# Landmark inverse: the symmetric product K V as its own stationary operand, its transposed product left out, the first bracket taken from the copy

## The reference

```python
def iterative_inv(K, n_iter=6):
    I = jnp.eye(K.shape[-1], dtype=K.dtype)
    denom = jnp.max(jnp.sum(K, axis=-2), axis=-1)[..., None, None]
    V = jnp.swapaxes(K, -1, -2) / denom
    for _ in range(n_iter):
        KV = K @ V
        V = 0.25 * V @ (13.0 * I - KV @ (15.0 * I - KV @ (7.0 * I - KV)))
    return V
...
SV = kernel1 @ iterative_inv(kernel2) @ (kernel3 @ V)
```

## Time and profile before

| | us |
|---|---|
| median of 3 runs | 6197.68 |
| lowest and highest of them | 6192.51 and 6201.0 |
| the profiled execution | 6204.73 |
| its span | 6202.7 |
| stage L2B in it, about | 2727 to 2842 |

### The profile page before, as it was taken

One profiled execution on the slowest core, in us unless ns is written; L12 is line 12 of the kernel. 1 busy time (PEld: TensorE's weight loads), 2 busy tenths in 40 slices (PEclk: granted clock), 3 DMA queues, 4 the chain that ended last, 5 costly groups with the idle time before them and its releaser, 6 DMA issues. The chain is left out here.

```text
span 6202.7 us, 126873 instructions
## 1 busy us (share of the span) xinstructions
PE 5537.1 (89%) x43980; PEld 3071.1 (50%) x43980; DVE 3363.8 (54%) x4908; ACT 2454.3 (40%) x3318; POOL 2574.7 (42%) x2473
## 2 busy tenths in 40 slices
PE   8569999999997798899689699999999978789996
PEld 6463333333335333779458233333333328778885
DVE  4237777777774697545553466666666634621112
ACT  2225555555552221333422355555555541122221
POOL 0036556555651396331301555555555530161032
PEclk9689999999999898999799899999999999789998
DMA  4863344434433422000026433333333347476675
GB/s 144 258 202 94 90 92 94 93 91 92 95 80 81 136 88 58 25 2 2 5 61 198 120 108 107 104 108 108 104 108 106 104 151 236 166 240 225 205 235 176
DMA packets 840068, 742.62 MB, mean 120 GB/s; under 512 B 514917, under 2 KB 722597, under 8 KB 828966
## 3 DMA queue, kind: packets, MB, share of 16 engines
q1 hardware_dynamic: 827302, 711.16, 39.5%
q0 software_dynamic: 12288, 25.18, 1.2%
HBM read 464.33 MB, written 278.00 MB: 120 GB/s over the span
## 5 line engine op out<-in xcount | busy, mean ns | idle before, releaser
L1186 DVE TENSOR_REDUCE L3B_nmax<-L3B_R 128x1 bf16<-128x1024 f32 x768 | 941.1, 1227 | 635.1 <-PE L3B_R L1080 635.1
L1186 DVE TENSOR_REDUCE L0B_nmax<-L0B_R 128x1 bf16<-128x1024 f32 x768 | 937.0, 1222 | 392.5 <-PE L0B_R L1080 378.5
L1172 ACT ACTIVATE L0B_PT<-L0B_R 128x1024 f32<-128x1024 f32 x768 | 786.6, 1025 | 671.7 <-PE L0B_R L1090 642.8
L1172 ACT ACTIVATE L3B_PT<-L3B_R 128x1024 f32<-128x1024 f32 x768 | 753.3, 1024 | 575.9 <-PE L3B_R L1090 575.9
L1090 PE MATMUL L0B_R<-L0B_QS,L0B_KS 64*128 64x512 bf16 (+1 forms) x6144 | 804.6, 382 | 45.8 <-issue 39.1
L1116 PE MATMUL L3B_O<-L3B_PT,L3B_VA 128*64 128x512 f32 x3072 | 743.6, 605 | 0.0
L1090 PE MATMUL L3B_R<-L3B_QS,L3B_KS 64*128 64x512 bf16 (+1 forms) x6144 | 730.8, 377 | 2.9 <-DMA L3B_QS<-scr_max 2.9
L1090 PEld LDWEIGHTS L0B_R<-L0B_QS,L0B_KS 64*128 64x128 bf16 (+1 forms) x6144 | 260.8, 94 | 511.1 <-issue 207.1
L1090 PEld LDWEIGHTS L3B_R<-L3B_QS,L3B_KS 64*128 64x128 bf16 (+1 forms) x6144 | 299.3, 94 | 329.7 <-ACT L3B_PT L1172 5.7
L1111 PE MATMUL L0B_O<-L0B_PT,L0B_VA 128*32 128x256 f32 x6144 | 422.1, 392 | 1.2 <-issue 1.0
L3236 ACT ACTIVATE L3F_hidden<-L3F_H,L3F_weights 128x256 f32<-128x256 f32 x474 | 182.1, 484 | 488.7 <-PE L3F_H L3168 488.7
(11 more groups left out here) (397 smaller groups left out, 8499.9 us busy)
## 6 DMA issues: line engine op xcount, KB each, us to landing
L3F_weights<-in_L3F_w SPq DMA_DIRECT2D x79, 1251.0 KB, 5.9
scr_sumsL<-L3B_OT SPq DMA_DIRECT2D x96, 512.0 KB
L3C_sums<-scr_sumsL SPq DMA_DIRECT2D x96, 512.0 KB, 9.4
scr_rel<-L0R_terms SPq DMA_DIRECT2D x64, 384.0 KB
L0B_raw<-scr_rel SPq DMA_DIRECT2D x192, 128.0 KB
L3B_raw<-scr_rel SPq DMA_DIRECT2D x384, 64.0 KB
scr_parts<-L0B_qk_parts SPq DMA_DIRECT2D x96, 224.0 KB, 2.3
scr_parts<-L3B_qk_parts SPq DMA_DIRECT2D x96, 224.0 KB, 2.2
```

Source lines behind the costliest of these rows:

```text
L1172: nc.scalar.activation(PT[:, (8 * u + j) % NPT, :, :], score_pair(u, j), ACT.Exp).then_inc(s_exp, 1)
L1186: nc.vector.tensor_reduce(nmax[:, u % 2, 4 * t:4 * t + 1], pair.rearrange("p j n -> p (j n)"), AX, ALU.max, negate=True).then_inc(s_mx, 1)
```

## The change

Product 1, the transposed K V, is left out. ScalarE copies product 0 instead, to `KV`, and `KV` is the stationary operand of the two products that had `KVT`. The first bracket is no longer made from PSUM but from that copy in SBUF, so VectorE waits for ScalarE and TensorE for VectorE there. An iteration has five products, numbered on through all iterations so that the two sets of PSUM banks go on taking turns. The hardware loops are written out: six times the body in the program's text, with constants in the waits.

```diff
-        def out(p, c):
-            return ps[:, p % 2, c, 0:GC * CG].rearrange("p (g n) -> p g n", g=GC)
+        def out(n, c):
+            return ps[:, n % 2, c, 0:GC * CG].rearrange("p (g n) -> p g n", g=GC)
+
+        def made(eng, n, c):
+
+            eng.wait_ge(s_pe, 2 * NC_ + NC_ * n + c + 1)
...
-            with pe.Fori(0, ITER) as it:
-                a0, d0 = it * 12, it * 12
+            for it in range(ITER):
+                n = 5 * it
                 for c in range(NC_):
-                    pe.wait_ge(s_a, a0 + 4 + c + 1)
-                    product(0, c, K2T, V)
+                    pe.wait_ge(s_a, 12 * it + 4 + c + 1)
+                    product(n, c, K2T, V)
                 for c in range(NC_):
-                    pe.wait_ge(s_a, a0 + 8 + c + 1)
-                    product(1, c, V, K2T)
+                    pe.wait_ge(s_a, 12 * it + 8 + c + 1)
+                    pe.wait_ge(s_d, 12 * it + c + 1)
+                    product(n + 1, c, KV, A)
                 for c in range(NC_):
-                    pe.wait_ge(s_a, a0 + 12 + c + 1)
-                    pe.wait_ge(s_d, d0 + 12 + c + 1)
-                    product(2, c, KVT, A)
+                    pe.wait_ge(s_d, 12 * it + 4 + c + 1)
+                    product(n + 2, c, KV, A)
                 for c in range(NC_):
-                    pe.wait_ge(s_d, d0 + 16 + c + 1)
-                    product(3, c, KVT, A)
+                    pe.wait_ge(s_d, 12 * it + 8 + c + 1)
+                    product(n + 3, c, VT, A)
                 for c in range(NC_):
-                    pe.wait_ge(s_d, d0 + 20 + c + 1)
-                    product(4, c, VT, A)
-                for c in range(NC_):
-                    product(5, c, A, VT)
+                    product(n + 4, c, A, VT)
...
-            with act.Fori(0, ITER) as it:
+            for it in range(ITER):
                 for c in range(NC_):
-                    act.wait_ge(s_pe, it * 24 + PRE + 4 + c + 1)
-                    nc.scalar.copy(chunk(KVT, c), out(1, c)).then_inc(s_a, 1)
-                for p, dst in ((4, V), (5, VT)):
+                    made(act, 5 * it, c)
+                    nc.scalar.copy(chunk(KV, c), out(5 * it, c)).then_inc(s_a, 1)
+                for p, dst in ((3, V), (4, VT)):
...
-            dve.sem_inc(s_d, 12)
-            with dve.Fori(0, ITER) as it:
-                for e, p in enumerate((0, 2, 3)):
+            def combine(c, src, e):
+                nc.vector.scalar_tensor_tensor(out=chunk(A, c), in0=src, scalar=-1.0, in1=bc(eyes[:, e, :], 1, GC),
+                                               op0=ALU.mult, op1=ALU.add).then_inc(s_d, 1)
+
+            for it in range(ITER):
+                for c in range(NC_):
+                    dve.wait_ge(s_a, 12 * it + 12 + c + 1)
+                    combine(c, chunk(KV, c), 0)
+                for p in (1, 2):
                     for c in range(NC_):
-                        dve.wait_ge(s_pe, it * 24 + PRE + 4 * p + c + 1)
+                        made(dve, 5 * it + p, c)
+                        combine(c, out(5 * it + p, c), p)
```

More of the change, by code:

```diff
@@ L2160, in landmark_inverse @@
         ps = st.ps("ps", [CG, 2, NC_, 512])
-        K2T, V, VT, KVT, A = (st.sb(n, [CG, NGRP, CG]) for n in ("K2T", "V", "VT", "KVT", "A"))
+        K2T, V, VT, KV, A = (st.sb(n, [CG, NGRP, CG]) for n in ("K2T", "V", "VT", "KV", "A"))
         eyes = st.sb("eyes", [CG, 3, CG])
@@ L2181, in _ @@
             sp.dma_start(own[:, :], cst["block1"]).then_inc(s_w, 16)
-        PRE = 2 * NC_
         @block.tensor
@@ L2194, in _, with product @@
                                  start=True, stop=True).then_inc(s_pe, 1)
-            def product(p, c, lhsT, rhs):
+            def product(n, c, lhsT, rhs):
                 for g in range(c * GC, (c + 1) * GC):
-                    mm = nc.tensor.matmul(out(p, c)[:, g - c * GC, :], lhsT[:, g, :], rhs[:, g, :], start=True, stop=True)
+                    mm = nc.tensor.matmul(out(n, c)[:, g - c * GC, :], lhsT[:, g, :], rhs[:, g, :], start=True, stop=True)
                 mm.then_inc(s_pe, 1)
-            with pe.Fori(0, ITER) as it:
-                a0, d0 = it * 12, it * 12
+            for it in range(ITER):
+                n = 5 * it
                 for c in range(NC_):
-                    pe.wait_ge(s_a, a0 + 4 + c + 1)
-                    product(0, c, K2T, V)
+                    pe.wait_ge(s_a, 12 * it + 4 + c + 1)
+                    product(n, c, K2T, V)
                 for c in range(NC_):
-                    pe.wait_ge(s_a, a0 + 8 + c + 1)
-                    product(1, c, V, K2T)
+                    pe.wait_ge(s_a, 12 * it + 8 + c + 1)
+                    pe.wait_ge(s_d, 12 * it + c + 1)
+                    product(n + 1, c, KV, A)
                 for c in range(NC_):
-                    pe.wait_ge(s_a, a0 + 12 + c + 1)
-                    pe.wait_ge(s_d, d0 + 12 + c + 1)
-                    product(2, c, KVT, A)
+                    pe.wait_ge(s_d, 12 * it + 4 + c + 1)
+                    product(n + 2, c, KV, A)
                 for c in range(NC_):
-                    pe.wait_ge(s_d, d0 + 16 + c + 1)
-                    product(3, c, KVT, A)
+                    pe.wait_ge(s_d, 12 * it + 8 + c + 1)
+                    product(n + 3, c, VT, A)
                 for c in range(NC_):
-                    pe.wait_ge(s_d, d0 + 20 + c + 1)
-                    product(4, c, VT, A)
-                for c in range(NC_):
-                    product(5, c, A, VT)
+                    product(n + 4, c, A, VT)
             for c in range(NC_):
-                pe.wait_ge(s_a, ITER * 12 + 8 + c + 1)
-                product(6, c, T3, VT)
+                pe.wait_ge(s_a, 12 * ITER + 8 + c + 1)
+                product(5 * ITER, c, T3, VT)
         @block.scalar
@@ L2240, in _ @@
                 i.then_inc(s_a, 1)
-            with act.Fori(0, ITER) as it:
+            for it in range(ITER):
                 for c in range(NC_):
-                    act.wait_ge(s_pe, it * 24 + PRE + 4 + c + 1)
-                    nc.scalar.copy(chunk(KVT, c), out(1, c)).then_inc(s_a, 1)
-                for p, dst in ((4, V), (5, VT)):
+                    made(act, 5 * it, c)
+                    nc.scalar.copy(chunk(KV, c), out(5 * it, c)).then_inc(s_a, 1)
+                for p, dst in ((3, V), (4, VT)):
                     for c in range(NC_):
-                        act.wait_ge(s_pe, it * 24 + PRE + 4 * p + c + 1)
-                        nc.scalar.mul(chunk(dst, c), out(p, c), 0.25).then_inc(s_a, 1)
+                        made(act, 5 * it + p, c)
+                        nc.scalar.mul(chunk(dst, c), out(5 * it + p, c), 0.25).then_inc(s_a, 1)
             for c in range(NC_):
-                act.wait_ge(s_pe, ITER * 24 + PRE + c + 1)
-                nc.scalar.copy(chunk(M2T, c), out(6, c)).then_inc(s_a, 1)
+                made(act, 5 * ITER, c)
+                nc.scalar.copy(chunk(M2T, c), out(5 * ITER, c)).then_inc(s_a, 1)
         @block.vector
```

2 lines of the change are left out of this document (removed).

## The result

| | before | changed |
|---|---|---|
| median of 13 runs, us | 6202.75 | 6186.54 |
| lowest and highest | 6187.91 and 6220.38 | 6178.58 and 6192.14 |
| ratio, 95% interval | | 0.9971 (0.9961 to 0.9982) |
| span of the profiled execution | 6202.7 | 6176.6 |
| L2B, first matmul to L2C's first | 113.49 | 102.10 |

By the ratio the changed kernel takes 0.29% less; between the medians it is 16.2 us (0.26%). The forecast time of 6186.6 was met to 0.1 us, and that closely only by luck: the gain was 16 us and not 11, and the median of before, with more runs, lies 5 us above the one I started from. The two errors cancel.

The account below looks back on a forecast made before the run. TensorE was taken to bound stage L2B. Terms: -13.6 (iterations 2 to 6) + 0 (first iteration) + 2.5 (clock) + 0 (loops written out) = -11.1 us, from 6197.68 to 6186.6 us; range 6179 to 6196.

Parts of the forecast that it names:

- What bounds the kernel: In L2B TensorE ends last and the other engines follow: six products an iteration, 2.72 us each, without a hole.
- The last rival: L2B not paced by TensorE, or drift elsewhere as large: the median stays at 6197.7 us; chance 0.03.
- Iterations 2 to 6: In L2B, the transposed product's 2.72 us falls out of each of five iterations: 13.6 us less.
- The slack beneath: In L2B's steady iterations, the first bracket's first chunk is ready 0.3 to 0.6 us before TensorE needs it.
- "bracket comes late" rival: In L2B, slower handoffs or SBUF brackets make TensorE wait each iteration: gain only 9 to 10.5 us; chance 0.09.
- The first iteration's own term of 0: In L2B's first iteration, 3.31 us of matmuls become 3.3 us of idle TensorE, waiting for ScalarE: no gain.
- The clock term: After the first iteration's hole in L2B, TensorE runs at half speed for longer: +2.5 us, bounds 0 and 3.1.
- The first rival: The clock is up when work resumes after L2B's hole, so 13.6 us are gained, 6184.1 us; chance 0.22.
- Code loading: In L2B, six to eight loads of written-out code stop TensorE, making the kernel slower than before; chance 0.06.
- what this stage loses comes off the time one for one: Stages run one after another behind barriers, so any time saved in L2B shortens the whole kernel equally.
- within 0.2%: Chance 0.61 that the whole kernel's time measures within 0.2% of before.
- faster: Chance 0.36 that the whole kernel gains more than 0.2%, 12.4 us, ending below 6185.3 us.

Follow-up runs that it names:

- the filled hole: Changed kernel plus 16 matmuls with unread result in the first iteration, behind product 0: 6184.5 us, ratio 0.9979; L2B 99.9 us.
- The third comparison: The changed kernel unaltered, measured again on another chip: median 6189.7 us against 6198.7 of before, ratio 0.9984; L2B 102.4 us.
- the loops written out: Kernel before with only its three hardware loops written out, still six products an iteration: median 6202.9 us against 6202.0, ratio 1.0000.
- my two failed expectations: Changed kernel with four unread products at L2B's end, then also a chunk of four matmuls: L2C 132.1 and 131.0 us, where 135.5 to 136 was expected.
- the first V made elsewhere: Changed kernel with VectorE making the first V and GpSimd the first VT instead of ScalarE: ratios to before 0.9968 and 0.9971; L2B 94.8 us.
- the bracket before the copy: Changed kernel with the first bracket made from PSUM again and ScalarE's copy to KV behind it: L2B 103.4, L2C 136.1 us.

## Why the prediction was right

- **What bounds the kernel** held: L2B is paced by TensorE, and the time followed it. The last rival (the change does less than it says) is out with that.
- **Iterations 2 to 6** gave 5 x 2.72 = 13.6 us to 0.01 us an iteration. The slack beneath, put at 0.3 to 0.6 us, measured 0.6; the bracket from SBUF at 0.55 was 0.554. The "bracket comes late" rival is out.
- **The first iteration's own term of 0** held within 0.1 us: the pair started 8.46 us behind product 0, where it had started 8.54 us behind it.
- **The clock term**, +2.5 with bounds 0 and 3.1, measured 2.2. The mechanism was right; the work resumed and the clock rose 4.8 us later, between the 4.3 and 6.5 I had read from before. The first rival (the clock does not suffer) is out by the filled hole. The third comparison had the state that it asks for, a clock that has risen ahead of the hole, and the clock fell in the hole all the same.
- **Code loading**, the rival on the other side, is out by the loops written out: ratio 1.0000, L2B 113.5 us.
- **What was missed** is a step of the first part: "what this stage loses comes off the time one for one". I took the clock into account inside L2B and treated everything behind it as merely shifted. But L2C, its code unchanged, had 13.7 us at half speed before and 6.8 after, and that was 3.6 us more of gain. The sum should have held -11.4 - 3.6 = -15.0, 6182.7 from the median that I used; that the time came out at 6186.5 is the luck with the median of before. The rows were there to ask: the clock's 0.50 at the head of L2C in the kernel before was readable. The size was not to be had from them, as my two failed expectations show. A bound was: half speed loses at most half of its time, so 13.7 us of it could give back 6.8 us at most.
- **The chances**: "within 0.2%" had 0.61 and "faster" 0.36. Measured 0.29%, 0.30% and 0.16% in three comparisons, 0.24% over all: it was the smaller chance that came.

## What to carry to other kernels

An instruction stream can hide another's latency and also keep TensorE's clock up. When a redundant product is taken out, cost the hole that it leaves twice: once in idle time and once in half speed behind it, here 0 and 2.2 us. Look also at the next stage: where its first matmuls fall against the clock's changes was worth up to 5.6 us in a stage that nobody touched, a third of what the change gave, so for differences under 0.1% compare the rows of the stage and the granted clock, not the whole time. If the hole is made by an engine's preparation, give that to idle engines, as the first V was here: 7.3 us of stage for eight operations.

## What the runs showed of the hardware

- The clock's pattern within the stages mostly repeated: in 9 of the 14 profiles the clock fell 7.4 to 7.7 us behind L2B's first matmul, in spite of start times that differed by 16 us, and L2B's length repeated to 0.1 us (113.5 and 113.5 with six products, with and without loops; 102.1, 102.1 and, in loops, 102.0 with five). Three profiles on another chip had the fall at 7.8 to 8.2 us, and the changed kernel there took 102.4; in the two with the first V made elsewhere it didn't fall there at all.
- A clock that is up can fall within one gap of TensorE: in the third comparison it had been at 1.00 for some 3 us, fell 2.4 us into the hole of 3.9 us, and came back 5.4 us after work had resumed.
- Where it differs, little decides: with the bracket before the copy the hole ended 0.6 us sooner and the stage was 1.3 us longer than the changed kernel's. With much the same idle time before L2C (1.59 us, and 1.26 in the two profiles with the first V made elsewhere), L2C started with the clock falling on its first matmul, 0.4 to 1.4 us into it, or 7.7 to 10.1 us into it, and took 136, 132 and 131 us.
- A TENSOR_TENSOR of 96 x 384 f32 in SBUF took VectorE 1020 ns while GpSimd ran its own at 1149 ns each, nearly twice the 554 ns of the bracket, another operation of the same size that ran alone. No run here has either of them without the other, so that one slows the other is open.
- A code load every 12 us (nine packets in 110 us) stays hidden behind a TensorE that takes 23.5 records a microsecond.
